# Two layers of gated cross attention: the nearest two prototypes sought in the products, rows moved two tiles at a time, and the fourth query product ahead of the attend

## The reference, cut to what matters

```python
x = x + tanh(g_xattn[1]) * L1_xattn(layernorm(x), ctx, ctx, Wq, Wk, Wv, Wo)
x = x + tanh(g_ffn[1]) * L1_ffn(layernorm(x), prototypes, B, A, bias, temp)

def L1_ffn(x, prototypes, B, A, bias, temp):      # 32 prototypes, rank 16
    d2 = sum(x*x) + sum(prototypes**2) - 2.0 * (x @ prototypes.T)
    dists = sqrt(maximum(d2, 0.0))
    w = softmax(-dists / t)
    topw, topi = top_k(w, 2)
    topw = topw / sum(topw)
    out = 0
    for slot in range(2):                          # the two nearest prototypes
        h = B[topi[slot]] @ x
        out += topw[slot] * (A[topi[slot]] @ h + bias[topi[slot]])
    return out
```

## Time and profile before

| | |
|---|---|
| median of 3 runs | 3044.14 us (3039.18 to 3046.79) |
| the profiled execution's own time | 3044.48 us |
| its span, first to last instruction | 3042.8 us |
| mean granted TensorE clock | 0.981 |
| busy: PE, DVE, POOL, ACT | 2739.6, 2507.4, 2089.8, 1983.7 us |

### The profile page before, as it was taken

One profiled execution on the slowest core, in us unless ns is written; L12 is line 12 of the kernel. 1 busy time (PEld: TensorE's weight loads), 2 busy tenths in 40 slices (PEclk: granted clock), 3 DMA queues, 4 the chain that ended last, 5 costly groups with the idle time before them and its releaser, 6 DMA issues.

```text
span 3042.8 us, 96434 instructions
## 1 busy us (share of the span) xinstructions
PE 2739.6 (90%) x31534; PEld 2166.8 (71%) x31534; DVE 2507.4 (82%) x6126; ACT 1983.7 (65%) x4683; POOL 2089.8 (69%) x2777
## 2 busy tenths in 40 slices
PE   4888896899999999689699999999989999999996
PEld 2444444677777777557578888888878888888885
DVE  6877776688888888675689999899989989999885
ACT  2666666687777877575466666666656666666663
POOL 3893000567666676544388888888888888888886
PEclk9999998899999999899899999999999999999998
DMA  5987566223233232631567766666776767766663
GB/s 152 364 337 294 235 254 256 76 81 93 77 90 84 80 93 76 220 117 41 121 142 158 158 147 149 140 145 150 145 137 149 141 144 149 147 150 145 145 132 78
DMA packets 638943, 455.55 MB, mean 150 GB/s; under 512 B 389760, under 2 KB 612592, under 8 KB 633648
## 3 DMA queue, kind: packets, MB, share of 16 engines
q1 hardware_dynamic: 618288, 402.31, 52.2%
q0 software_dynamic: 7328, 23.40, 2.5%
q10 hardware_dynamic: 12960, 25.23, 2.2%
HBM read 235.08 MB, written 148.83 MB: 126 GB/s over the span
## 4 chain that ended last, share of the span: by engine, by line
PE 32%; DVE 6%; issue 4%; POOL 3%; SPq 2%; ACT 2%; DMA 1%; DVEq 0%; POOLq 0%; ACTq 0%
PE banks L150 10%; PE banks L152 9%; PE banks L151 9%; PE banks L1416 2%; DVE a_near L1540 2%; PE banks L1401 2%; SPq L1058 1%; DVE a_probT_lo L1492 1%; ACT a_qT_hi L1234 1%; DVE a_pick L1627 1%; DVE a_rsum L1504 1%; DVE a_wtop L1567 1%; POOL a_pn L1154 1%; DMA a_xnT<-a_xn_parts 0%; DMA a_hwT<-a_hw_parts 0%
## 5 line engine op out<-in xcount | busy, mean ns | idle before, releaser
L1234 ACT ACTIVATE a_qT_hi<-banks 128x512 f16<-128x512 f32 x252 | 150.4, 597 | 540.8 <-PE banks L152 540.8
L383 POOL TENSOR_TENSOR a_probT_lo<-a_expT,a_probT_hi 128x512 f16<-128x512 f32 x256 | 291.4, 1159 | 218.5 <-ACT a_probT_hi L466 218.5
L459 ACT ACTIVATE a_expT<-banks,a_top,w_score_scale 128x512 f32<-128x512 f32 (+1 forms) x384 | 272.4, 709 | 152.5 <-PE banks L550 146.1
L1154 POOL TENSOR_TENSOR a_pn<-a_prob,a_rsum 128x1024 f32<-128x1024 f32 (+1 forms) x256 | 310.2, 1233 | 5.8 <-DVE a_rsum L1506 5.8
L150 PE MATMUL banks<-a_xnT,w_q_hi 128*128 128x256 f16 x1024 | 281.2, 275 | 15.0 <-DMA a_xnT<-a_xn_parts 13.2
L150 PE MATMUL banks<-a_vo_front,a_probT_hi 128*128 128x256 f16 x1024 | 279.8, 273 | 9.4 <-DVE a_probT_lo L1492 6.5
L152 PE MATMUL banks<-a_xnT,w_q_lo 128*128 128x256 f16 x1024 | 280.6, 274 | 0.0
L151 PE MATMUL banks<-a_xnT,w_q_hi 128*128 128x256 f16 x1024 | 280.6, 274 | 0.0
L152 PE MATMUL banks<-a_vo_front,a_probT_lo 128*128 128x256 f16 x1024 | 279.7, 273 | 0.0
L151 PE MATMUL banks<-a_vo_front,a_probT_hi 128*128 128x256 f16 x1024 | 279.6, 273 | 0.0
L1490 DVE TENSOR_TENSOR a_qT_lo<-banks,a_qT_hi 128x512 f16<-128x512 f32 x252 | 172.0, 683 | 77.9 <-ACT a_qT_hi L1234 77.7
(11 more groups left out here) (380 smaller groups left out, 10177.7 us busy)
## 6 DMA issues: line engine op xcount, KB each, us to landing
vo<-kv_vo_out SPq DMA_DIRECT2D x38, 2048.0 KB, 8.1
a_vo_front<-vo SPq DMA_DIRECT2D x128, 512.0 KB
kt<-kv_k_out ACTq DMA_DIRECT2D x9, 2560.0 KB, 14.9
a_k<-kt SPq DMA_DIRECT2D x64, 308.0 KB, 3.5
kv_raw_e<-in_L_ffn_w POOLq DMA_DIRECT2D x16, 1024.0 KB, 8.9
a_x<-in_x SPq DMA_DIRECT2D x64, 256.0 KB, 2.9
a_y<-in_x SPq DMA_DIRECT2D x64, 256.0 KB, 2.7
x<-a_y SPq DMA_DIRECT2D x64, 256.0 KB, 2.8
```

The costliest lines, as they stand in the source:

```text
L383: pool.tensor_tensor(probT[b][1][:, first:end, :], expT[b][:, first:end, :], probT[b][0][:, first:end, :], ALU.subtract).then_inc(prob_rea ...
L459: act.activation(expT[1 - h][0:rows, first:end, :], bank, ACT.Exp, bias=top[0:rows, 0:1], scale=weights["score_scale"][0:rows, 0:1]).then_ ...
L1154: last = pool.tensor_tensor(keys_of(pn[h]), e[:, :, first:end], rsum[h][:, :].unsqueeze(2).broadcast_to([P, H, end - first]), ALU.mult)
L1234: act.activation(out, bank[:, 0:cols].rearrange("p (c s) -> p c s", c=out.shape[1]), ACT.Copy, scale=scale)\
```

## The change

In layer 1, four things are different.

- The two nearest prototypes are sought in the products `dots` themselves. The squared length of a row is the same for all prototypes, so it doesn't change their order. `near` is gone; `max` and `max_index` read `dots`. The squared distances of the two found are made by a new ACT instruction, `square_gaps`: relu(ysq - top), 128x2. POOL adds TINY to it where it multiplied by -1 before, and waits for ACT (`gap_ready`). `ysq` has four places in the place of two.
- `square_gaps` of tile t-6 stands on ACT between the first probability group and `norm2_log`. It waits for `top_found`, which DVE signals near the end of the tile before.
- The rows are loaded, and the results stored, for two tiles in one DMA of 256 KB; `y_sb` has 16 slots in 8 pairs.
- The fourth query product of a batch goes ahead of the attend of h=1 (`prep(4)`), on PE and in the ring of banks, and its low half ahead of `add_residual` on DVE. On ACT its place is the same.

```diff
-    SLOTS = 8
+    SLOTS = 16
+    PAIRS = SLOTS // TPB
     PROBS = 4
     LU = 2
+    LENGTHS = 4
...
-    SUM_STEPS, TOP_STEPS = 2, 3
+    SUM_STEPS, TOP_STEPS = 2, 4
...
-            for n, number in enumerate((-0.5, 0.5, -1.0, 1.0)):
+            for n, number in enumerate((-0.5, 0.5, TINY, 1.0)):
...
-    y_sb = [sb(f"y{s}", [P, D]) for s in range(SLOTS)]
+    y_pair = [sb(f"y{s}", [P, TPB, D]) for s in range(PAIRS)]
+    y_sb = [y_pair[s // TPB][:, s % TPB, :] for s in range(SLOTS)]
...
-    ysq = sb("ysq", [P, TPB])
+    ysq = sb("ysq", [P, LENGTHS])
...
-        at = {(0, 2): [("q", 0)], (0, 3): [("q", 1)], (1, 0): [("q", 2)], (1, 2): [("q", 3)]}
+        at = {(0, 2): [("q", 0)], (0, 3): [("q", 1)], (1, 0): [("q", 2)], (1, 4): [("q", 3)]}
...
             names += of(7, [("wselT", h)])
+            names += prep(4)
             names += of(3, [("out", h)])
...
-        def load_rows(t, slot, before):
-
-            need(sp, out_done[slot], before * 16)
-            sp.dma_start(y_sb[slot][:, :], src_rows[tile_at(t)]).then_inc(y_in[slot], 16)
+        def load_rows(i, slot, before):
+
+            pair = slot // TPB
+            need(sp, out_done[pair], before * 16)
+            sp.dma_start(y_pair[pair][:, :, :], src[batch_at(i)]).then_inc(y_in[pair], 16)
...
-                t = i * TPB + h - LAG
-                if live(i * TPB + h - 2, NT):
-                    load_rows(i * TPB + h - 2, *place(2, u, h, j))
+                if h == 0 and live(i - 1, NB):
+                    load_rows(i - 1, *place(2, u, 0, j))
...
-                if live(t, NT):
-                    slot = (TPB * u + h - LAG) % SLOTS
-                    need(sp, out_ready, t + 1)
-                    sp.dma_start(dst[tile_at(t)], y_sb[slot][:, :]).then_inc(out_done[slot], 16)
+                if h == 1 and live(i - LAG // TPB, NB):
+                    pair = (u - LAG // TPB) % PAIRS
+                    need(sp, out_ready, (i - LAG // TPB + 1) * TPB)
+                    sp.dma_start(dst[batch_at(i - LAG // TPB)], y_pair[pair][:, :, :]).then_inc(out_done[pair], 16)
...
-            need(pool, top_used, t)
-            pool.tensor_tensor(dist[:, :], top[:, 0:2], numbers[:, 2:3].broadcast_to([P, 2]), ALU.mult).then_inc(top_used, 1)
+            need(pool, gap_ready, t + 1)
+            kept = pool.tensor_tensor(dist[:, :], square[:, :], numbers[:, 2:3].broadcast_to([P, 2]), ALU.add)
             pool.tensor_copy(topf[:, :], topi[:, 0:2]).then_inc(top_ready, 1)
-            need(pool, top_used, t + 1)
+            step(kept)
...
+        def square_gaps(t, h, u):
+
+            n = (TPB * u + h - 6) % LENGTHS
+            need(act, top_found, t + 1)
+            need(act, ysq_done, t + 1)
+            need(act, more_ready, t)
+            act.activation(square[:, :], top[:, 0:2], ACT.Relu, bias=ysq[:, n:n + 1], scale=-1.0).then_inc(gap_ready, 1)
...
-            need(act, near_ready, t - 1)
-            act.activation(ysq[:, h:h + 1], inv2[:, :], ACT.Identity, scale=mv2[:, 1:2]).then_inc(ysq_done, 1)
+            act.activation(ysq[:, n:n + 1], inv2[:, :], ACT.Identity, scale=mv2[:, 1:2]).then_inc(ysq_done, 1)
...
                     if g == 0:
                         prep(0)
+                        if live(t - 6, NT):
+                            square_gaps(t - 6, h, u)
                         if live(t - 4, NT):
                             norm2_log(t - 4)
...
+                prep(4)
                 if live(t - 3, NT):
                     attend(i, t - 3, h, u, j)
                 prep(2)
...
-            need(dve, near_ready, t)
+            need(dve, topi_found, t)
...
-        def nearest_two(t, h):
-
+        def nearest_two(t):
+
+            need(dve, gap_ready, t)
             need(dve, dots_read, t + 1)
-            need(dve, ysq_done, t + 1)
-            nc.vector.tensor_scalar(near[:, :], dots[:, :], ysq[:, 1 - h:2 - h], -TINY, ALU.subtract, ALU.min)\
-                .then_inc(near_ready, 1)
-            need(dve, top_used, t)
-            hold(near_ready, t + 1)
-            nc.vector.max(top[:, :], near[:, :]).then_inc(top_found, 1)
+            nc.vector.memset(idle_top[:, :], 0.0)
+            nc.vector.max(top[:, :], dots[:, :]).then_inc(top_found, 1)
...
-            nc.vector.max_index(topi[:, :], top[:, :], near[:, :]).then_inc(topi_found, 1)
+            nc.vector.max_index(topi[:, :], top[:, :], dots[:, :]).then_inc(topi_found, 1)
...
+                prep(4)
                 if live(t - 3, NT):
                     add_residual(i, t - 3, h, u, j)
```

More of the change, by code:

```diff
@@ L773, in attention_ffn_phase @@
     vo_in = [sem(f"vo_in{p}") for p in range(2)]
-    out_done = [sem(f"out_done{s}") for s in range(SLOTS)]
-    y_in = [sem(f"y_in{s}") for s in range(SLOTS)]
+    out_done = [sem(f"out_done{s}") for s in range(PAIRS)]
+    y_in = [sem(f"y_in{s}") for s in range(PAIRS)]
     work_full = [sem(f"work_full{s}") for s in range(WORK)]
@@ L792, in attention_ffn_phase @@
         sem("yn_ready"))
-    ln_log, ln_root, more_ready, first_weight = sem("ln_log"), sem("ln_root"), sem("more_ready"), sem("first_weight")
+    gap_ready, ln_log, ln_root, more_ready, first_weight = sem("gap_ready"), sem("ln_log"), sem("ln_root"), sem("more_ready"), sem("first_weight")
     ln2_inverse = sem("ln2_inverse")
     yn_hi, yn_lo, dots_read = sem("yn_hi"), sem("yn_lo"), sem("dots_read")
[L796 to L799, removed]
+    top_found, topi_found, top_ready = sem("top_found"), sem("topi_found"), sem("top_ready")
+    top_step, wtops_ready, picked, wsel_ready = (
+        sem("top_step"), sem("wtops_ready"), sem("picked"), sem("wsel_ready"))
     low_ready, hw_ready, hw_hi, hw_lo, wselT_hi, wselT_ready, out_ready = (
@@ L952, in attention_ffn_phase @@
     ynT = [sb(f"ynT{p}", [P, 2 * DC, P], F16) for p in range(2)]
-    ysq = sb("ysq", [P, TPB])
-    dots, near = sb("dots", [P, NPROTO]), sb("near", [P, NPROTO])
+    ysq = sb("ysq", [P, LENGTHS])
+    dots, idle_top = sb("dots", [P, NPROTO]), sb("idle_top", [P, 1])
     top, topi, topf = sb("top", [P, 8]), sb("topi", [P, 8], U32), sb("topf", [P, 2])
-    dist, dgap, late, wtop = sb("dist", [P, 2]), sb("dgap", [P, 1]), sb("late", [P, 1]), sb("wtop", [P, 2])
+    dist, square, dgap, late, wtop = sb("dist", [P, 2]), sb("square", [P, 2]), sb("dgap", [P, 1]), sb("late", [P, 1]), sb("wtop", [P, 2])
     more, euler, decay = sb("more", [P, 1]), sb("euler", [P, 1]), sb("decay", [P, 1])
@@ L1127, in _ @@
         bodies(sp, body)
-        for s in range(SLOTS):
-            sp.wait_ge(out_done[s], 16 * (NT // SLOTS))
+        for s in range(PAIRS):
+            sp.wait_ge(out_done[s], 16 * (NB // PAIRS))
     @block.gpsimd
@@ L1276, in norm2_shift, with length2 @@
             act.activation(inv2[:, :], rstd2[:, :], ACT.Square, scale=math.sqrt(D)).then_inc(ln2_inverse, 1)
-        def length2(t, h):
+        def length2(t, h, u):
+            n = (TPB * u + h - 4) % LENGTHS
             need(act, ln2_inverse, t + 1)
-            need(act, near_ready, t - 1)
-            act.activation(ysq[:, h:h + 1], inv2[:, :], ACT.Identity, scale=mv2[:, 1:2]).then_inc(ysq_done, 1)
+            act.activation(ysq[:, n:n + 1], inv2[:, :], ACT.Identity, scale=mv2[:, 1:2]).then_inc(ysq_done, 1)
         def rows_high(i, u, j):
@@ L1340, in body @@
                                    scale=rstd2[:, 0:1]).then_inc(yn_ready, 1)
-                    length2(t - 4, h)
+                    length2(t - 4, h, u)
                     normed_high(t - 4, u, h, j)
@@ L1572, in add_residual @@
             slot, before = place(3, u, h, j)
-            need(dve, y_in[slot], (before + 1) * 16)
+            need(dve, y_in[slot // TPB], (before + 1) * 16)
             nc.vector.scalar_tensor_tensor(out=y_sb[slot][:, :], in0=bank[:, 0:D], scalar=out_scale,
@@ L1638, in body @@
                 if live(t - 5, NT):
-                    nearest_two(t - 5, h)
+                    nearest_two(t - 5)
                     nearest_index(t - 5)
@@ L2961, in flamingo_layers @@
             wq, score_scale, ffn = weights1.results()
-            layer1 = attention_ffn_phase(nc, layer, psum, const, batches(x1), tiles(x1), tiles(out), keys(DC, KV_COLS // P),
+            layer1 = attention_ffn_phase(nc, layer, psum, const, batches(x1), tiles(x1), batches(out), keys(DC, KV_COLS // P),
                                          (out_front, out_back), wq, score_scale, ffn,
```

## The result

The changed kernel takes 3051.9 us (median of 12 runs, 3046.39 to 3054.22), the kernel before 3044.35 in the same session (12 runs, 3039.18 to 3050.31). The ratio is 1.0022, 95% interval 1.0013 to 1.0031: slower by 7 to 8 us, less than the 0.3% that the prediction took as the bound of "no change". The profiled execution took 3054.22 us; it was the slowest of the twelve, so the two profiles are 9.7 us apart where the medians are 7.6.

What follows compares the result with a forecast made beforehand. PE's own work plus one chain, E to the attend of h=0, was taken as the bound: 23.60 - 6.66 + 7.02 = 23.96 us, +0.22 on 23.74, some 60 batches, +13: 3057 us (3044 to 3072; 8 in 10: 2994 to 3072).

Steps and rivals of the forecast that it cites:

- Part 1: Fourth query product ahead of the attend: PE's 0.66 us wait before the scores goes; what depends on the attend starts 1.31 later.
- Part 2: SBUF port shared by DVE and POOL: near's 0.9 us wait passes to the second pick, which waits out POOL's 1.24 us instruction.
- Part 3: New ACT wait: square_gaps waits for top_found, so the attend of h=0 comes 7.02 us after E, where it was 6.66.
- floor of 5.5: PE's own work from E to the attend of h=0 without any wait: under 5.5 us.
- The list of signs: Signs if right include PE waiting about 0.9 us before the second down product and 1 us before the attend of h=0.
- Part 4: Rows and results two tiles per DMA on SP: taken as 0, with under 1 us added for the last store.
- The sum: New batch period 23.96 us against the mean of 23.74: +0.22, over some 60 batches +13 us.
- Rival 1: Both DVE picks pass before POOL's instruction; attend at 6.05, -0.75 us a batch, 2999 us; chance 0.28.
- Rival 2: No change: blocked pick and ACT's wait eat the gain, attend at 6.8 after E; 3044 us, 3035 to 3053; chance 0.2.
- Rival 3: A second wait of PE in h=1, for pn or a bank, 0.5 us more a batch; 3087 us; chance 0.07.

Runs made afterwards that it cites:

- e1: The changed kernel with the fourth query product back behind the attend of h=1; 3077.44 us, ratio 1.0089 against the kernel before.
- e3: The kernel before with only the loads and stores of two tiles in one DMA; 3042.47 us, ratio 0.9986.
- e5: The changed kernel with POOL's low half of xn_parts moved behind weigh; 3019.49 us, ratio 0.9926 against the kernel before.
- e4: The changed kernel with square_gaps behind ACT's third split in both tiles; 3031.94 us, ratio 0.9941 against the kernel before.
- e6: The changed kernel with the edits of e5 and e9 together; 3007.75 us, ratio 0.9880 against the kernel before.
- e10: e2 with POOL's low half of xn_parts behind weigh (near and one-tile DMAs kept); 3039.54 us, ratio 0.9982 against the kernel before.
- e2: The kernel before with only the fourth query product moved ahead of the attend of h=1; 3048.51 us, ratio 0.9995.
- e13: The kernel before with the fourth query product ahead of the attend and two-tile DMAs, near kept; 3040.48 us, ratio 0.9987.
- e9: The changed kernel with square_gaps behind ACT's third split in h=0 only; 3015.65 us, ratio 0.9916 against the kernel before.
- e12: e9 with SP's loads of a batch's values dealt over both tiles; 3043.61 us, ratio 0.9992 against the kernel before.

## Why the prediction came out as it did

It said 3057 us and slower; measured 3051.9, inside the forecast's own range of 3044 to 3072. The steps, in us from E, the start of PE's transposes (2654.24 in the rows above):

| step | predicted | measured |
|---|---|---|
| residual, bn_stats | 0.20, 0.72 | 0.21, 0.73 |
| quarter sum | 0.66 to 1.40 | 0.67 to 1.40 |
| last sum on POOL | 1.47 to 2.09 | 1.48 to 2.09 |
| low half of xn_parts from | 2.05 | 2.05 |
| end of the second pick | 3.33 | 3.24 |
| wsel, max | 3.36, 3.56 | 3.28, 3.46 |
| square_gaps, norm2_log | 3.80, 3.99 | 3.69, 3.89 |
| third split | 6.05 | 5.95 |
| attend of h=0 | 7.02 | 6.99 |
| period | 23.96 | 23.98 mean, 23.97 here |

- **Part 1 held.** No wait stands before the scores any more, and xn_parts was ready before POOL could take it.
- **Part 2 held.** POOL's phase, which no row of before showed in the new order, came out to 0.01 us, and near's wait passed to the second pick. One small reading was wrong and cost nothing: wtop didn't wait out the quarter sum until 1.41 but began 0.1 later, at 1.39, and took 0.13, so the first pick began at 1.55 for 1.45; POOL sets its end either way. L1164 took 1.15 where the step had 1.24 from one row; that is the 0.1 by which all behind it is earlier. The Trainium skill (SBUF — State Buffer, Who interferes with whom) says that a DVE instruction with two SBUF inputs contends with a GpSimd instruction that reads SBUF; e1 agrees, wsel taking 1.18 us for 0.26 beside L1164. bn_stats with its one input took 0.43 beside the quarter sum, the same as in the kernel before, where it ran ahead of it.
- **Part 3 held.** ACT waited 2.44 us; square_gaps put off its successor by 0.20, where the step had 0.19. PE's waits were 0.59 and 0.84, 1.43 in all, about what 6.99 less the floor of 5.5 leaves. The list of signs had 0.9 and 1; both were too high, and their sum of 1.9 didn't fit the prediction's own 7.02 less 5.5.
- **Part 4, counted at 0, was nearly so.** The steady batches don't feel the two-tile DMAs (e3: 23.79 for 23.81).
- **The sum** was too high by the term of the old period. 23.74 was the mean of 27 late batches; over 56 it is 23.81, since the earlier ones are longer. With it the step gives 56 x 0.15 = 8 us; 9.7 were measured in the batches. The rest of the batch, 23.60 - 6.66 = 16.94 in the sum, is 16.96 and 16.97 in the two kernels. The one chain of 6.66 that the prediction read is among the shortest of the kernel before, whose chains run from 6.64 to 7.30 with the median at 6.80; in the changed kernel nearly all are at 6.98 (6.97 to 7.28). So the step is 0.17 at the mean, not the 0.36 between 6.66 and 7.02. The long batch, which no step had, gave 3.2 back, and the two ends of the layer took 3.1: that these cancel is luck.

**The rivals.** Rival 1 (both picks pass) didn't occur: the second pick is long in nearly every batch, as ACT's 49 waits show. e5, which lets the second pick pass by other means, has the attend at 6.07 where rival 1 had 6.05, but gives 3019 where rival 1 had 2999: the transposes come late and the rest of the batch grows. Rival 1 didn't have that. Rival 2's time (3044) is nearly as close as the forecast's, but its mechanism, the attend settling at 6.8 after E, isn't what the rows show: 6.8 is the median of the kernel before, and the changed one stands at 6.98. Rival 3 was seen in e4 only.

What stays open: the batch of 25.7 to 29.9 us in the middle of the layer; which of the search and the two-tile DMAs makes e6 faster than e10; and why the transposes land later with the loads dealt over both tiles.

## What to carry to other kernels

Removing an instruction that is long only because it waits doesn't remove the wait: find the other engine's instruction that it waits out, and ask who will stand there next. Here near, the first pick, the second pick or wsel paid for the same POOL instruction in four orders. Moving that one was worth 29 and 34 us with the search, where moving q3 alone gave nothing clear of noise and the two-tile DMAs alone 4, and the search cost 11 to 31. It was worth only 4 without the search, where the transposes behind it took the gain back: so look also at what the moved instruction itself feeds. And a new consumer of a late result belongs behind the work on its engine that others wait for: moving the added ACT instruction behind the last split, in one tile of two, gave 32 us.

## What the runs showed of the hardware

- POOL gets in between two DVE instructions that follow each other closely: between the two picks here, whose own lengths are some 0.3 us, between wtop and the first pick in e2, and 0.09 us ahead of wsel in e1. In no stretch shown here did DVE run two such instructions in a row while POOL's stood ready.
- Removing PE's waits for transposes can be worth next to nothing: 20.4 us of them went from e2 to e13, the waits for the splits grew by 22.8, and the ratios, 0.9995 and 0.9987, can't be told apart.
- Transposes on the same queue took 2.3 to 3.4 us from issue to landing in e9 and 2.9 to 4.1 in e12, with the same transfers in another order.
